# Last image in two token halves, filler products on PE in a bank of their own, and a new order of work

## Chip, cores and metric

The kernel runs on one core of a Trainium2 chip. The metric is device time in microseconds (us). Before the change the median of three runs is 472.86 us (471.47 to 474.82).

## The reference, cut to what matters

Four images of 16x16 tokens with 128 channels go through three layers one after another: a deformable attention layer, an attention layer over segments, and a layer of product-key experts. The change touches the end of the third:

```
s0 = einsum(l2norm(q0), l2norm(keys0)); s1 = the same with q1, keys1   # 8 heads, 64 keys a side
sc0, ix0 = top_k(s0, 16);  sc1, ix1 = top_k(s1, 16)
fs, pos  = top_k(all sums sc0 + sc1, 16);  fi = ix0 + ix1 at pos       # expert numbers below 128
w   = softmax(fs)
act = gelu(x . expert_down[fi])
out = sum over heads and k of act * w * expert_up[fi];   t = t + out
```

## The kernel before, in words

An image b has 256 tokens in two halves of 128 (t = 0, 1). Its work is cut into some sixty named stages (A: first layer, F: the rest of it and the second, N: experts). Each engine walks its own written list of `stage.image` (`ORDERS`, L108 to L142), strictly in order; images overlap because the lists interleave them. A stage on one engine waits on semaphores for what another engine made. Results of PE go into eight PSUM banks; the string `BANKS` (L154) gives each PE job its bank in the order of PE's list, and a job waits until the bank's last reader has freed it (`take`, L501).

Stages that the prediction speaks of:

- F7b: the layer norm statistics of the first layer's result (DVE L1172 and statistics), whose inverse root POOL takes (L1497). A2a to A2b2: POOL's multiplications and folds of the next image's convolution (L454, L1529).
- F9b, F9c: attention scores, four banks each, reduced by DVE (L1201). F10a, F10b: scores again, four banks each (PE L708), exponentials on ACT (L1003). F11a: the weighted sum (PE L721), F11t and F11b transposes, F11c projection. F5a: first-layer scores of the next image (PE L587). A1b: its query projection (PE L544).
- N0a, N0h: query projections of halves 0 and 1. N0b, N0d: their transposes (PE L520, ACT L1035). N0c, N0e: key scores (PE L775, ACT L1045). N1_0 to N1_3: the best keys on DVE (L1317 to L1327), two stages a half.
- N2a to N2f: the sixteen chosen pairs of each half. DVE sums and marks (L1365 to L1376) and masks (`chosen`, L1383 to L1389); POOL makes the sums of indices and of exponentials (`cells`) and merges the cells into 27 slots a head (`merge`, L1614 to L1620). L1389 multiplies 1/sum by 2^15.
- N3a: PE transposes the slots of both halves, weights (wT) and expert numbers (eT); ACT copies them (L1082, L1084); DVE splits the numbers in low and high bits (L1419, L1420), takes the remainder of the weights (L1425), makes four low masks (L1428) and four masked weight rows R (L1432). N3b: 32 masks of the high bits, 28 on DVE (L1437) and 4 on POOL (L1647).
- N5a, N5b: for each half PE adds the slots into experts, 128 pairs of a weight load (108x128, half precision) and a 16-column product (L839); DVE multiplies by the activations (L1442). N4 makes these activations. N6a: product with the up matrix (PE L850), ACT copy, N6b: transposes, the addition on DVE (L1459), and the store by DMA.

For the last image nothing of another image is left after N2f, so N3a to N6b run there one behind the other.

Of the kernel before, what the change touches and what calls it, by code (L numbers as in the profile page):

```python
# [52 lines left out]
POOL_HI = 4  # L53
W_SCALE = 2.0 ** 15
# [54 lines left out]
    "tensor": """A1a.0 A1b.0 A2d.0 A3a.0 A3b.0 A3c.0 A4.0 F5a.0 A1a.1 F5c.0 A1b.1 NS.0 F6a.0 F6b.0 F6c.0 F7a.0 F7b.0  # L109
        F8a.0 F8b.0 A2d.1 F9b.0 F9a.0 F8c.0 A3a.1 A3b.1 F9c.0 A3c.1 A4.1 F9d.0 F10a.0 F10b.0 F5a.1 F11a.0 A1a.2  # L110
        F11t.0 F11b.0 F11c.0 F5c.1 F12.0 N0a.0 F6a.1 N0h.0 F6b.1 A1b.2 N0b.0 F6c.1 N0c.0 N0d.0 N0f.0 F7a.1 F7b.1
        F8a.1 F8b.1 F8c.1 F9b.1 N0g.0 N0e.0 F9a.1 N4.0 A2d.2 A3a.2 F9c.1 A3b.2 F9d.1 A3c.2 F10a.1 A4.2 F10b.1
        F11a.1 F5a.2 F11t.1 F11b.1 F11c.1 N3a.0 F12.1 F5c.2 N0a.1 N0h.1 F6a.2 A1a.3 F6b.2 F6c.2 N0b.1 N0c.1
        N0d.1 N5a.0 N0e.1 F7a.2 N0f.1 F7b.2 N0g.1 N5b.0 F8a.2 F8b.2 A1b.3 F8c.2 F9b.2 F9a.2 F9c.2 A2d.3 N4.1
        N6a.0 F9d.2 A3a.3 A3b.3 A3c.3 F10a.2 F10b.2 F11a.2 A4.3 F11t.2 N6b.0 F11b.2 F5a.3 F11c.2 N3a.1 F5c.3
        F12.2 N0a.2 N0h.2 F6a.3 F6b.3 N0b.2 F6c.3 N0f.2 N0c.2 N0d.2 N0e.2 N5a.1 F7a.3 F7b.3 N5b.1 F8a.3 N4.2
        F8b.3 N0g.2 F8c.3 F9b.3 F9a.3 N6a.1 F9c.3 F9d.3 F10a.3 F10b.3 F11a.3 N6b.1 F11t.3 F11b.3 F11c.3 N3a.2
        F12.3 N0a.3 N0h.3 N0b.3 N0c.3 N0f.3 N5a.2 N0d.3 N0e.3 N0g.3 N5b.2 N6a.2 N4.3 N6b.2 N3a.3 N5a.3 N5b.3
        N6a.3 N6b.3""".split(),
    "scalar": """A0b.0 A1a.0 A2c.0 A2d.0 A3a.0 A1b.0 A3b.0 A3c.0 A4.0 A0b.1 F5b.0 A1a.1 F5c.0 F6b.0 F7a.0 F7b.0 A2c.1  # L120
        F8a.0 F8b.0 A1b.1 A2d.1 F9a.0 A3a.1 A3b.1 A3c.1 A4.1 A0b.2 F8c.0 F10a.0 F10b.0 F11t.0 A1a.2 F11b.0 F5b.1
        F12.0 F5c.1 N0a.0 F6b.1 N0h.0 N0b.0 N0c.0 F7a.1 F7b.1 N0d.0 F8a.1 F8b.1 A2c.2 F8c.1 N2p.0 A2d.2 F9a.1
        N0e.0 A3a.2 A3b.2 A3c.2 N2q.0 A1b.2 F10a.1 A4.2 F10b.1 F11t.1 F11b.1 N3a.0 F5b.2 F12.1 F5c.2 N0a.1 N0h.1
        A0b.3 F6b.2 N0b.1 N0c.1 N0d.1 A1a.3 N4.0 F7a.2 N0e.1 F7b.2 F8a.2 F8b.2 F8c.2 F9a.2 A2c.3 A2d.3 N2p.1
        A3a.3 A3b.3 A3c.3 F10a.2 F10b.2 N2q.1 A1b.3 F11t.2 N6a.0 A4.3 F11b.2 F5b.3 N3a.1 F12.2 F5c.3 N0a.2 N0h.2
        F6b.3 N0b.2 N0c.2 N0d.2 N4.1 F7a.3 F7b.3 N0e.2 F8a.3 N4.2 F8b.3 F9a.3 N2p.2 N2q.2 F10a.3 F8c.3 F10b.3
        N6a.1 F11t.3 F11b.3 N3a.2 F12.3 N0a.3 N0h.3 N0b.3 N0c.3 N0d.3 N0e.3 N2p.3 N2q.3 N6a.2 N4.3 N3a.3 N6a.3""".split(),
    "vector": """A0a.0 A2c.0 A3a.0 NB.0 A0a.1 F5a.0 NS.0 F6a.0 F6c.0 F7b.0 A2c.1 F8b.0 F9b.0 F9a.0 F9c.0 A0a.2 F9d.0
        F5a.1 A3a.1 F11a.0 F11c.0 N0a.0 F6a.1 N0b.0 N0h.0 F6c.1 N0d.0 N1_0.0 F7b.1 N1_1.0 A2c.2 N0f.0 F8b.1
        F9b.1 A3a.2 N2a.0 N2b.0 N1_2.0 F9a.1 N0g.0 F9c.1 N1_3.0 F9d.1 N2d.0 N2c.0 N2e.0 N2f.0 F11a.1 A0a.3 F5a.2  # L130
        F11c.1 N3a.0 N3b.0 N0a.1 F6a.2 N0h.1 N0b.1 N0d.1 F6c.2 N1_0.1 N1_1.1 N0f.1 N1_2.1 F7b.2 N2a.1 N2b.1
# [1590 lines left out]
```

## Time and profile before

| what | value |
|---|---|
| median of 3 runs | 472.86 us |
| profiled execution | 472.43 us, of it the span 470.6 us |
| PE busy | 296.5 us, 63% |
| weight loads on PE | 219.8 us, 47% |
| DVE busy | 356.8 us, 76% |
| ACT busy | 137.3 us, 29% |
| POOL busy | 220.8 us, 47% |
| granted PE clock, mean | 0.675 |
| chain that ended last | DVE 49%, PE 33%, ACT 7%, issue 5%, POOL 5% |

The span is the profiled stretch on the core; 1.8 us of the execution lie outside it. A busy share is an average over stages with different limits, so the rows further down are read stage by stage. The granted clock is 1.00 for 2.4 GHz and 0.50 for 1.2 GHz. The chain is followed back from the last instruction, at each step to what released it.

### The profile page before, as it was taken

The page shows a single profiled execution, that of the slowest core. Times are in us where ns is not written, and L with a number is a line of the kernel's source. Part 1 is how long each engine was busy: PE and PEld are TensorE (multiplying, and loading weights), DVE is VectorE, ACT ScalarE, POOL GpSimd, SP SyncE. Part 2 cuts the span into 40 slices and gives each one's busy share as a digit, 9 for nine tenths or more (in the row PEclk, how much of TensorE's full clock was granted, in tenths as well). Part 3 has the DMA queues.
Part 4 walks back from the last instruction along what each step waited for, and adds up shares of the span by engine and source line. Part 5 has one row for each costly group of instructions (what it writes and reads, how often), then busy time and mean ns, then how long its engine had stood idle before and what let it go on. Part 6 is the DMA issues. An engine that isn't in the chain of part 4 may idle for free.

```text
span 470.6 us, 7700 instructions
## 1 busy us (share of the span) xinstructions
PE 296.5 (63%) x2233; PEld 219.8 (47%) x2233; DVE 356.8 (76%) x2124; ACT 137.3 (29%) x320; POOL 220.8 (47%) x407
## 2 busy tenths in 40 slices
...
DMA packets 1633, 3.50 MB, mean 7 GB/s; under 512 B 180, under 2 KB 1205, under 8 KB 1592
## 3 DMA queue, kind: packets, MB, share of 16 engines
...
q8 instruction: 18, 0.29, 0.3%
...
HBM read 2.49 MB, written 0.52 MB: 6 GB/s over the span
## 4 chain that ended last, share of the span: by engine, by line
DVE 49%; PE 33%; ACT 7%; issue 5%; POOL 5%; DVEq 0%; ACTq 0%; POOLq 0%
PE bank L839 9%; DVE cands L1376 4%; DVE segmax L1201 4%; PE bank L520 4%; DVE onehot L1437 3%; DVE Sx L1320 3%; PE bank L755 3%; PE bank L775 3%; DVE i L1326 3%; DVE i L1327 3%; DVE c L1373 3%; DVE vraw L1323 2%; DVE rtm L1193 2%; DVE vraw L1317 2%; PE bank L608 2%
## 5 line engine op out<-in xcount | busy, mean ns | idle before, releaser
L839 PE MATMUL bank<-weights,onehot 108*128 108x16 f16 x1024 | 68.6, 216 | 18.5 <-DVE onehot L1437 13.0
L839 PEld LDWEIGHTS bank<-weights,onehot 108*128 108x128 f16 x1024 | 68.7, 175 | 19.4 <-DVE onehot L1437 13.5
L1584 POOL TENSOR_TENSOR inv<-nrm,mhalf 128x16 f32<-128x16 f32 x8 | 24.2, 3019 | 46.9 <-DVE nrm L1333 46.8
L454 POOL TENSOR_TENSOR taps<-qpad,wa 128x128 f32<-128x128 f32 x96 | 35.9, 425 | 17.4 <-ACT qpad L892 17.4
L1497 POOL TENSOR_TENSOR rstd<-veps,mhalf 128x2 f32<-128x2 f32 x16 | 11.7, 729 | 44.0 <-DVE veps L1123 43.7
L1647 POOL TENSOR_SCALAR onehot<-eT 108x512 f16<-108x512 uint16 x16 | 30.2, 1888 | 4.2 <-DVE eT L1420 3.5
L1437 DVE TENSOR_SCALAR onehot<-eT 108x512 f16<-108x512 uint16 x112 | 28.1, 327 | 0.0
L1326 DVE FIND_INDEX8 i<-vraw,S 128x8 uint16<-128x64 f32 x128 | 28.0, 219 | 0.0
L1327 DVE FIND_INDEX8 i<-vraw,Sx 128x8 uint16<-128x64 f32 x128 | 28.0, 219 | 0.0
L708 PE MATMUL bank<-qB,kE 32*128 32x256 f32 x128 | 16.3, 663 | 18.0 <-ACT PT L1003 10.1
L775 PE MATMUL bank<-KB,qsT 128*128 128x256 f32 x64 | 24.4, 548 | 3.5 <-ACT qsT L1035 3.5
L1320 DVE MATCH_REPLACE8 Sx<-vraw,S 128x64 f32<-128x64 f32 x128 | 25.1, 209 | 0.0
L1573 POOL TENSOR_TENSOR qrstd<-ssq,mhalf 128x8 f32<-128x8 f32 x8 | 17.7, 2212 | 14.7 <-DVE ssq L1285 14.7
L1376 DVE MATCH_REPLACE8 cands<-c,cands 128x54 f32<-128x54 f32 x128 | 23.7, 199 | 0.0
L520 PE MATMUL bank<-wa,hat 128*128 128x128 f32 x24 | 7.4, 406 | 24.8 <-ACT hat L877 24.6
L1317 DVE MAX8 vraw<-S 128x8 f32<-128x64 f32 x128 | 17.7, 213 | 6.3 <-ACT S L1045 6.3
L1201 DVE TENSOR_REDUCE segmax<-bank 128x32 f32<-128x512 f32 x32 | 19.8, 681 | 2.5 <-PE bank L678 2.4
L775 PEld LDWEIGHTS bank<-KB,qsT 128*128 128x128 f32 x64 | 17.2, 283 | 8.1 <-ACT qsT L1035 4.9
L1602 POOL TENSOR_TENSOR weights<-ab 128x64 f32<-128x64 f32 (+3 forms) x40 | 12.6, 348 | 17.9 <-ACT ab L1065 17.9
L1529 POOL TENSOR_TENSOR taps<-taps 128x1536 f32<-128x1536 f32 (+3 forms) x12 | 20.6, 1714 | 0.6
L1442 DVE TENSOR_TENSOR masked<-bank,act 128x512 f32<-128x512 f32 x8 | 8.4, 1072 | 16.0 <-PE bank L839 15.9
L708 PEld LDWEIGHTS bank<-qB,kE 32*128 32x128 f32 x128 | 10.0, 319 | 22.1 <-issue 12.0
...
## 6 DMA issues: line engine op xcount, KB each, us to landing
...
bq_row<-rows_dram SPq DMA_DIRECT2D x1, 0.5 KB
...
```

Source lines behind the costliest of these rows:

```text
L454: ins = eng.tensor_tensor(tv[:, :, :, ky, kx:kx + n], q, dw[:, ky, kx:kx + n].unsqueeze(1).unsqueeze(1).broadcast_to([P, G8, G8, n]), ALU. ...
L708: last = mm(banks[i][:, kc * N:kc * N + N], kE[r, j, kc * P:kc * P + P], qB[r, j, :], start=True, stop=True)
L775: last = mm(o[:, i * 256:i * 256 + 256], qsT[:, t, 2 * j + i, :], KB[:, :], start=True, stop=True)
L839: last = mm(o[:, g * 16:g * 16 + 16], OHv[:, c * NT + t, g], Rv[:, c, t, g, s], start=(c == 0 and s == 0), stop=(c == NCH - 1 and s == 1))
L1201: freed(v.tensor_reduce(segmax[:, t * H + i:t * H + H:4, :], o[:, :].rearrange("p (g n) -> p g n", n=SEG), X, ALU.max), job, b)
L1317: last = v.max(vt[:, g, 0:8], sv[:, g, :])
L1320: last = v.match_replace(sx[:, g, :], vt[:, g, 0:8], sv[:, g, :], MARK)
L1326: v.max_index(it[:, g, 0:8], vt[:, g, 0:8], sv[:, g, :])
L1327: last = v.max_index(it[:, g, 8:16], vt[:, g, 8:16], sx[:, g, :])
L1376: last = v.match_replace(dst[:, g, :], c8[:, g, i, :], src[:, g, :], MARK)
L1437: last = v.tensor_scalar(OH[0:KC, :, :, hi, :], hi_view(eT), float(LO * hi), None, ALU.is_equal)
L1647: last = g_.tensor_scalar(OH[0:KC, :, :, hi, :], hi_view(eT), float(LO * hi), None, ALU.is_equal)
```

## The change

1. All four lists are written anew; the stages are the same but for the additions. Among the moves: on PE, F5a.1 goes from before F11a.0 to behind F11t.0, A1a.2 from before F11t.0 to behind F11c.0, A1b.2 from before N0b.0 to behind F9b.1, N0d.3 from behind N5a.2 to before it, N5b.1 to directly behind N5a.1. On ACT, F8c.0 goes before the stage A4.1 and A0b.2 behind F11t.0. On POOL, F7b.0 goes before the last folds A2b2.1. On DVE, N5b.2 goes before N2a.3 and N6b.2 before N2e.3.
2. `W.0` to `W.20` in PE's list: two products each of 128x128 by 512 columns in bf16 of a tile of ones, into bank 7, which nobody reads. The other jobs get banks 0 to 6.
3. For the last image N3a and N3b do token half 0 alone; the new N3h and N3i do half 1. On PE N3h stands before N5a.3; on POOL the order is N3b.3, N2f.3 (the merge of half 1), N3i.3. The rows R of a half are eight operations of 256 columns in place of four of 1024.
4. The scale 2^15 moves from L1389, which goes, into ACT's copy and DVE's remainder, an operation that each does already.
5. `prod`, which DVE writes at L1442 and PE streams at L850, is laid out as DVE reads its operands; PE now reads it with a step of 16 elements.

```
-        f"... F9d.0 F10a.0 F10b.0 F5a.1 F11a.0 A1a.2 F11t.0 F11b.0 F11c.0 F5c.1 F12.0 N0a.0 ..."
+        f"... W.7 W.8 F8c.0 F9d.0 W.9 F10a.0 F10b.0 F11a.0 F11t.0 F5a.1 F11b.0 F11c.0 A1a.2 F5c.1 F12.0 N0a.0 ..."
...
+        "N5a.2 N0f.3 N0e.3 W.15 N5b.2 N0g.3 W.16 N6a.2 W.17 N4.3 N6b.2 N3a.3 N3h.3 N5a.3 W.18 N5b.3 W.19 W.20 N6a.3 N6b.3"
...
+            def W(k):
+                if k == 0:
+                    pe.wait_ge(preset, 1)
+                for _ in range(FILL):                     # FILL = 2
+                    mm(psum[7][:, :], ones3[:, :], ones3[:, :].unsqueeze(1).broadcast_to([P, 4, P]), start=True, stop=True)
...
+        def first_halves(b):
+            return list(range(NT)) if b < B - 1 else [0]
...
             def F8c(b):
                 o = take("v1", b)
+                read_out(pe, "tT", b)
...
+            def slot_transposes(b, halves, job):
+                pe.wait_ge(slots_ready, NT * b + halves[-1] + 1)
+                for kind, src in (("w", wn[:, :, :]), ("e", slots[:, 1, :, :])):
+                    transposes(kind + job, b, [
+                        ((c * NT + t) * P, src[:, t * H + c * HC:t * H + (c + 1) * HC, :].rearrange("p h s -> p (h s)"))
+                        for c in range(NCH) for t in halves])
...
             def N5b(b):
+                if b == B - 1:
+                    pe.wait_ge(onehot_dve_ready, b + 2)
+                    pe.wait_ge(onehot_pool_ready, b + 2)
                 scatter(b, 1)
...
+                pv = prod[:, :, :, :].rearrange("p t g (q l) -> p l t q g", q=4)
-                    last = mm(o[:, 0:N], up[:, lo, :], prod[:, lo], start=(lo == 0), stop=(lo == LO - 1))
+                    last = mm(o[:, 0:N], up[:, lo, :], pv[:, lo], start=(lo == 0), stop=(lo == LO - 1))
...
-                link(v.reciprocal(zs[:, 1, h], zs[:, 0, h]))
-                v.tensor_scalar(zs[:, 2, h], zs[:, 1, h], W_SCALE, None, ALU.mult).then_inc(wem_ready, 1)
+                v.reciprocal(zs[:, 1, h], zs[:, 0, h]).then_inc(wem_ready, 1)
...
+            def slot_rows(b, halves, job):                # DVE, in place of the body of N3a
+                ...
+                for lo in range(LO):
+                    if len(halves) == NT:
+                        v.tensor_tensor(R[0:KC, :, lo, :], W2[0:KC, :, :],
+                                        lom[0:KC, lo, :].unsqueeze(1).broadcast_to([KC, 2, NCH * N]), ALU.mult)
+                    else:
+                        for s in range(2):
+                            v.tensor_tensor(part(R[0:KC, s, lo, :], halves), part(W2[0:KC, s, :], halves),
+                                            part(lom[0:KC, lo, :], halves), ALU.mult)
...
                 freed(v.tensor_tensor(
-                    prod[:, :, t, :, :].rearrange("p l q g -> p g q l"),
-                    o[:, :].rearrange("p (g q l) -> p g q l", g=32, q=4), act[:, t, :, :, :], ALU.mult), f"G{t}", b)
+                    prod[:, t, :, :], o[:, :].rearrange("p (g e) -> p g e", g=32),
+                    act[:, t, :, :, :].rearrange("p g q l -> p g (q l)"), ALU.mult), f"G{t}", b)
...
+            def N3i(b):                                   # POOL; DVE's has hi from POOL_HI to HI
+                pool.wait_ge(eT_ready, b + 2)
+                for hi in range(0, POOL_HI):
+                    last = masks(g_, hi, [1])
+                last.then_inc(onehot_pool_ready, 1)
```

## Rows read from the trace of the kernel before

**Rows 1.** Windows of all engines: window, us, busy (count) of PE, PEld, DVE, ACT, POOL, clock

```profile
0.00:120.00 120.00, 66.25 (x316) 41.73 (x316) 62.61 (x246) 45.11 (x110) 65.03 (x129) 0.79 0.06 21
120.00:430.00 310.00, 207.06 (x1644) 157.04 (x1645) 279.39 (x1838) 90.65 (x207) 149.46 (x274) 0.65 0.01 3
430.00:470.60 40.60, 23.19 (x274) 21.06 (x273) 14.79 (x42) 1.58 (x3) 6.35 (x4) 0.50 0.01 4
```

**Rows 2.** Timeline of the head: start, us, engine, line, operation [idle before it]

```profile
55.64 1.55 DVE L1172 TENSOR_TENSOR t<-gl,z 128x256 f32<-128x256 f32 x1 [5.12 <-ACT gl L963]
80.42 0.88 ACT L877 ACTIVATE hat<-x_sb,shift,rstd 128x128 f32<-128x128 f32 x2 [5.61 <-POOL shift L1498]
83.01 4.03 ACT L1003 ACTIVATE PT<-bank 128x512 f32<-128x512 f32 x8
83.86 2.92 PE L587 MATMUL bank<-kBD,qhT 128*128 128x512 f32 x4
106.11 1.06 PE L544 MATMUL bank<-qT,wa 128*128 128x256 f32 x2
```

**Rows 3.** Timeline of DVE near 306: L1172 without POOL's folds beside it

```profile
306.72 0.42 DVE L1172 TENSOR_TENSOR t<-gl,z 128x256 f32<-128x256 f32 x1 [0.52 <-ACT gl L963]
```

**Rows 4.** Windows with the clock: the head's cold stretch, and inside a scatter

```profile
46.50:65.20 18.70, 8.52 (x25) 5.41 (x26) 4.77 (x17) 5.68 (x11) 12.48 (x20) 0.50 0.00 1
206.00:210.00 4.00, 4.00 (x63) 4.00 (x63) 3.97 (x39) 1.88 (x6) 3.84 (x11) 0.50 0.01 4
```

**Rows 5.** Timeline 379 to 393: last image's half 1 queries

```profile
379.29 8.56 PE L839 MATMUL bank<-weights,onehot 108*128 108x16 f16 x128 [5.51 <-issue]
388.83 0.78 ACT L1035 ACTIVATE qsT<-bank,wb 128x512 f32<-128x512 f32 x1 [15.20 <-PE bank L520]
392.46 1.11 DVE L1317 MAX8 vraw<-S 128x8 f32<-128x64 f32 x8 [4.50 <-ACT S L1045]
```

**Rows 6.** Lines L1442, L1291, L1389 alone: count, ns min/median/max, starts

```profile
L1442 DVE TENSOR_TENSOR masked<-bank,act x8: 1010/1042/1191, 232.1 to 461.8; 128x512 f32<-128x512 f32 x8
L1291 DVE TENSOR_TENSOR queries<-bank,qrstd x8: 672/682/692, 104.0 to 380.2; 128x512 f32<-128x512 f32 x8
L1389 DVE TENSOR_SCALAR zs<-zs x8: 170/171/260, 168.2 to 426.5; 128x8 f32<-128x8 f32 x8
```

**Rows 7.** Timeline of the tail: from the last merge to the product with the up matrix

```profile
426.69 0.53 POOL L1614 COPY slots<-masked 128x16 f32<-128x16 f32 x3 [0.74 <-DVE zs L1389]
429.21 0.55 POOL L1620 TENSOR_TENSOR wn<-slots,zs 128x216 f32<-128x216 f32 x1
432.56 0.29 DVE L1419 TENSOR_SCALAR eT<-eT 108x512 uint16<-108x512 uint16 x1 [5.60 <-ACT eT L1084]
435.02 3.26 DVE L1432 TENSOR_TENSOR weights<-W,cands 108x1024 f16<-108x1024 f16 x4
438.20 6.55 DVE L1437 TENSOR_SCALAR onehot<-eT 108x512 f16<-108x512 uint16 x28
444.80 16.98 PE L839 MATMUL bank<-weights,onehot 108*128 108x16 f16 x256 [13.04 <-DVE onehot L1437]
462.95 3.75 PE L850 MATMUL bank<-masked,up 128*128 128x256 f32 x8 [1.16 <-issue]
```

**Rows 8.** Timeline of DVE: eight searches over 54 columns

```profile
421.84 1.01 DVE L1373 MAX8 c<-cands 128x8 f32<-128x54 f32 x8
```

**Rows 9.** Timeline: DVE's masks and POOL side by side, image 2 and last image

```profile
364.87 1.64 POOL L1573 TENSOR_TENSOR qrstd<-ssq,mhalf 128x8 f32<-128x8 f32 x1 [5.36 <-DVE ssq L1285]
367.00 6.22 POOL L1573 TENSOR_TENSOR qrstd<-ssq,mhalf 128x8 f32<-128x8 f32 x1 [0.49 <-DVE ssq L1285]
367.44 5.74 DVE L1437 TENSOR_SCALAR onehot<-eT 108x512 f16<-108x512 uint16 x28
433.21 6.54 POOL L1647 TENSOR_SCALAR onehot<-eT 108x512 f16<-108x512 uint16 x4 [3.46 <-DVE eT L1420]
```

**Rows 10.** Waits of PE after 120 us: us in total, times, longest

```profile
PE bank L708 <- ACT PT L1003: 10.1, 3, 7.8
```

More of the change, by code:

```diff
@@ L53 @@
 POOL_HI = 4
+FILL = 2
 W_SCALE = 2.0 ** 15
@@ L108 @@
 ORDERS = {
[L109 to L118, printed above, removed]
-        N6a.3 N6b.3""".split(),
@@ L120 @@
[L120 to L131, printed above, removed]
-        N0g.1 A2c.3 N5a.0 N5b.0 F8b.2 F9b.2 F9a.2 F9c.2 N2c.1 F9d.2 N1_3.1 N2d.1 N2e.1 F11a.2 N2f.1 N6b.0 F5a.3
-        F11c.2 N3a.1 N0a.2 N0h.2 F6a.3 N0b.2 N3b.1 N0d.2 F6c.3 N1_0.2 N1_1.2 N5a.1 F7b.3 N0f.2 N1_2.2 N2a.2
-        N5b.1 N2b.2 F8b.3 F9b.3 F9a.3 F9c.3 N0g.2 N2c.2 F9d.3 A3a.3 N1_3.2 N2d.2 N2e.2 N2f.2 N6b.1 F11a.3 F11c.3
-        N3a.2 N0a.3 N0h.3 N0b.3 N3b.2 N1_0.3 N0d.3 N1_1.3 N1_2.3 N0f.3 N5a.2 N1_3.3 N0g.3 N2a.3 N5b.2 N2d.3
-        N2b.3 N2c.3 N2e.3 N2f.3 N6b.2 N3a.3 N3b.3 N5a.3 N5b.3 N6b.3""".split(),
@@ new lines @@
+    "vector": """A0a.0 A2c.0 A3a.0 NB.0 A0a.1 F5a.0 NS.0 F6a.0 F6c.0 F7b.0 A2c.1 F8b.0 F9b.0 F9a.0 F9c.0 F9d.0 A0a.2
+        F11a.0 F5a.1 F11c.0 N0a.0 F6a.1 N0b.0 N0h.0 F6c.1 N0d.0 N1_0.0 N1_1.0 N1_2.0 N0f.0 F7b.1 N1_3.0 A2c.2
+        N2a.0 N0g.0 F8b.1 F9b.1 F9a.1 F9c.1 N2b.0 F9d.1 N2d.0 N2c.0 N2e.0 N2f.0 F11a.1 F5a.2 A0a.3 F11c.1 N3a.0
+        N3b.0 N0a.1 F6a.2 N0h.1 N0b.1 N0d.1 F6c.2 N1_0.1 N1_1.1 N0f.1 N1_2.1 F7b.2 N2a.1 A2c.3 N5a.0 N2b.1 N5b.0
+        F8b.2 F9b.2 F9a.2 F9c.2 N2c.1 N0g.1 F9d.2 N1_3.1 N2d.1 N2e.1 F11a.2 N2f.1 F5a.3 N6b.0 F11c.2 N3a.1 N0a.2
+        N0h.2 A3a.1 F6a.3 N0b.2 N3b.1 A3a.2 N1_0.2 N0d.2 F6c.3 N0f.2 A3a.3 N1_1.2 N5a.1 N2a.2 N5b.1 F7b.3 N1_2.2
+        F8b.3 N2b.2 N0g.2 F9b.3 F9a.3 F9c.3 N2c.2 F9d.3 N1_3.2 N2d.2 N2e.2 N2f.2 F11a.3 N6b.1 F11c.3 N3a.2 N0a.3
+        N0h.3 N0b.3 N3b.2 N0d.3 N1_0.3 N1_1.3 N0f.3 N1_2.3 N1_3.3 N0g.3 N5a.2 N5b.2 N2a.3 N2d.3 N2b.3 N2c.3
+        N6b.2 N2e.3 N2f.3 N3a.3 N3b.3 N3h.3 N3i.3 N5a.3 N5b.3 N6b.3""".split(),
```

132 lines of the change are left out of this document (85 added, 47 removed).

## The prediction

> **What bounds the kernel now.** I read the shares first, then the windows, because DVE's 76% is an average over three very different stretches [rows 1]. Up to 120 us DVE is busy for 62.6 us: only image 0 and the front of image 1 are there, and their stages follow each other across the engines. From 120 to 430 us DVE is busy 279.4 of 310 us, 90%: here DVE is the bound, and what is taken off it or closes one of its gaps counts. From 430 us to the end it is 14.8 of 40.6 us: one image, one chain. So I read each stretch by another question: what stands ahead of the next link (head), what DVE does or waits for (middle), how much of the chain can run beside itself (tail).
>
> **Head.** (a) The addition L1172 of image 0 takes 1.55 us while POOL folds, 0.42 us without folds [rows 2, 3]. With F7b.0 ahead of the last folds, POOL stands idle meanwhile: 1.1 us less. The folds end some 3 us later; their reader on DVE stands before F8b.0, which waits for two more steps on ACT and PE, so they stay hidden. (b) ACT begins the exponentials of F10a.0 at 83.01, behind a layer norm of another image at 80.42 (0.88) and then 1.7 us of F8c's copy and a table load [rows 2]. In the new list both stages are away, and the load falls in an idle time. At most 2.6 us are to be had; PE's own products then come last, so I take 1.6 for the exponentials, which end near 85.5 instead of 87.0. F5a.1 (2.92 us, until 86.8) is no longer before F11a.0 either, and F11a.0 ends 2.0 us earlier. (c) A1a.2 leaves the place before F11t.0 (0.6 us) and A1b.2 that before N0b.0 (1.06 us [rows 2], 0.85 of it in the way); F5a.1 now stands between F11t.0 and F11b.0, in a gap that I estimate at 0.8 us, and costs 1.2 (warm) to 2.1 (cold); I take 1.6. Net 0.1 lost. (d) The fillers. They matter if they keep the clock at 1.00. From 46.5 to 65.2 us PE is busy 8.52 us at 0.50, on the chain [rows 4]; at full clock that is at best half, 4.2 us less. W.4 and W.5 stand before F6c.0, behind a step of ACT of half a us, and are four products of 512 columns, 0.85 us warm and 1.7 cold at a column a cycle of the granted clock. So (d) lies between 3.4 gained and 1.3 lost; I take 1.5 gained, since no row shows how soon they act. Head: 1.1 + 2.0 - 0.1 + 1.5 = **4.5 us**.
>
> The rest of the fillers I cost at nothing before the tail: W.0 to W.3, W.6 to W.8 and W.10 to W.17 stand before products that wait longer than the 0.85 us that a pair takes cold. Where that cover is missing a pair costs 0.85.
>
> Here a rule disagrees with a row. The clock is 0.50 from 206 to 210 us although PE's records fill all 4.0 us with 16-column products [rows 4]: being busy did not keep the clock. The Trainium skill ("TensorE: Matmul & The Clock Gate", What's actually happening) says that the default is throttled and activity releases it. By that rule alone all fillers pay and (d) is 3.4; the row says that the kind of work counts, so I do not take it whole.
>
> **Middle.** DVE's product L1442 writes scattered and takes 1.04 us; L1291, the same shape from PSUM with a packed output, 0.68 [rows 6]. I price the packed L1442 at 0.68: 0.36 off each, six in this stretch, 2.2 us (at worst nothing, if the scattered write is not the reason). L1389 (0.17 and its hand-over, 0.2 together) goes seven times before the last: 1.4 us. The scale moves into operations that exist, at no cost. Before the last image's N1_2, DVE stands idle 4.50 us, since N0d.3 starts behind the scatter that ends at 387.85; that scatter itself had waited 5.51 us [rows 5]. With N0d.3 before N5a.2 the transposes and ACT's copy fall into that wait, and the time from 387.85 to the copy's end at 389.61 goes: 1.8 us. Middle: 2.2 + 1.4 + 1.8 = **5.4 us**. The remaining moves shuffle work under a busy DVE; N5b.1 right behind N5a.1 makes F7a.3 and N0e.2 wait 8.6 us longer, but DVE has N1_1.2, N2a.2 and two products, over 12 us, ahead of them. I take zero for them, bounds 5 either way: DVE's idle time in this stretch is 30 us, most of it the small gaps between instructions.
>
> **Tail.** Before, N2f ends, POOL merges from 426.69 to 429.76, PE and ACT bring the slots to DVE at 432.56; DVE needs until 444.75 (2.46 for the first seven operations, 3.26 for R, 6.5 for the masks), PE 17.0 for both scatters, and from the product L850 to the end of the span are 7.65 us [rows 7].
> Half 0's mask was done at 421.84 [rows 8], now some 0.7 earlier by a cheaper product and L1389; its merge takes 3.1 to 4 and is done by 425.3, the transposes take 1.0, the copies 0.6: DVE can start N3a.3 at 427.0, 5.5 us earlier. N6b.2's early place frees the buffer that ACT's copy needs.
> Half of it on DVE: a mask over half the columns lies between 0.10 and 0.205 us; eight searches over 54 columns take 1.01 us, 0.126 each [rows 8], so little below that is to be had: I take 0.14, 28 are 3.9. R as eight operations of 256 columns: 1.6 (a quarter each) to 3.2; 1.9. The first seven: 1.7. With 1.3 for POOL's interference: 8.8 us, ready at 435.8. The split is no saving on DVE, it is 5.4 us more work; what it buys is that the second half lies beside the first scatter.
> POOL: the four masks of N3b.3 now stand before the merge of half 1. Masks of half the size are half of 6.54, 3.3 us [rows 9], the merge 3.1 to 3.8: slots near 434.4, transposes until 435.4. PE has N3h.3 before N5a.3, so the scatter of half 0 waits for that too; it starts at 435.8 and ends at 444.3. Half 1's preparation runs 436.3 to 444.1 beside it. W.18 is then not covered: 0.85. Scatter 1 ends at 453.7. W.19 and W.20 are four products, 1.7 us cold, where PE waits 1.1 us: product L850 starts at 455.4. I give it no warm clock, since after 17 us of scatter it is 0.50 [rows 1]. With 7.65 to the end the span ends at 463.0: **7.6 us**.
>
> **Sum.** 4.5 + 5.4 + 7.6 = 17.5. The profiled execution took 472.43, 0.43 under the median; 472.43 - 17.5 = 454.9, against the median 455.4. I say 455.
>
> **Rivals.** (1) *POOL is shut out in the tail.* Beside 28 masks of DVE in 5.74 us, a POOL instruction of 1.6 us took 6.22 [rows 9]: DVE went at full speed and POOL stood. Against it: in the last image POOL's four masks ran 6.54 us and DVE was the slower. If DVE wins in the new tail, POOL does its masks after 433.8, the merge ends at 440.2, half 0's scatter starts at 441.2, half 1 is ready at 452.3, and the span ends at 470.2: the tail gives 0.4 instead of 7.6, **462 us**. The Trainium skill ("SBUF — State Buffer", SBUF: two separate sides) calls this port pair an exclusive lock that whoever starts first holds for its instruction. The rows show both outcomes, so it decides nothing between them.
> (2) *Product L850 becomes slow.* Its moving operand has a step of 64 bytes now. If each column then costs twice, the last one adds 3.75 us, the three others lie beside DVE: **459 us**. Against it: a scatter pair loads 128 weight columns of half precision, 64 bytes apart, and streams 16 more in 66 ns (8.56 us/128), 2 columns a ns, where L850 needs one in 1.8 ns. The Trainium skill ("SBUF — State Buffer", The DMA port swizzle) has a rule that speaks for it: lines of 16 bytes, and two hits a line are needed for full speed.
> (3) *The clock is kept.* Fillers hold it in the head and at the end: 1.9 more in (d), and 2 to 3 elsewhere in the head and at L850: **450 us**.
> (4) *Seven banks are too few: slower.* F10a and F10b need eight banks; today PE already waits up to 7.8 us for one held by ACT [rows 10]. With seven, the last product of F10b, or of F9c, waits for the first reader, which in the middle comes when its engine's list lets it, and everything behind on PE waits with it, N0 products for DVE too. At 7.8 us on DVE's path for each of images 1 to 3 that is 23.4 us: **478 us**. It outweighs the gains from 6 us an image on. Against it: DVE and ACT read these sets in a row, 0.6 us a bank, so the fourth waits little.
> (5) *The new order gives back the gains* by milder waits of the same sort, 4 us an image: **467 us**.
>
> **Numbers.** Forecast (451 to 459 with its own bounds) 0.45, (1) 0.15, (2) 0.10, (3) 0.12, (4) 0.06, (5) 0.12. Range 446 to 468: it takes in all but (4) and parts of the edges. A measurement of this kernel tells about 1% from no change, 468.1 and 477.6. Faster: all but (4) and half of (5), less a little of (1): 0.84. Same 0.10, slower 0.06.
>
> **What would show it.** Head: L1172 of image 0 at 0.42, first exponentials near 79 to 80 on the new time axis, first N1_0 some 5 us earlier; the clock between 45 and 65. Middle: L1442 at 0.7, the idle before N1_2.3 under 3 us, no long wait of PE for a bank. Tail: scatter of half 0 starting 9 us before today's 444.8, a gap under 1.5 us between the scatters, L850 at 3.75. I am wrong if DVE's idle time in the middle grows, if POOL's merge of half 1 lands after 437, or if L850 lengthens.

## The result, and the profile after

The changed kernel takes 451.19 us (median of 4 runs, 449.87 to 452.28) against 473.58 (471.47 to 474.82) for the kernel before in the same comparison: ratio 0.953, 95% interval 0.949 to 0.958. The prediction said 455 with a range of 446 to 468. The profiled execution took 449.87 us, of it the span 447.8: 22.8 us less than the 470.6 of before, where the sum had said 17.5.

Three stretches as in [rows 1]: cut at 120 us again, and at 415 us, which lies 3.2 us behind the last 1/sum (430 lay 3.8 us behind it). Busy times of the engines, then the granted clock.

```profile
0.00:120.00 120.00, 72.25 (x350) 46.11 (x350) 66.95 (x307) 45.72 (x112) 62.77 (x127) 0.82 0.06 21
120.00:415.00 295.00, 211.26 (x1649) 158.11 (x1649) 275.93 (x1781) 93.82 (x209) 147.14 (x269) 0.67 0.01 3
415.00:447.80 32.80, 24.60 (x276) 20.96 (x276) 15.56 (x77) 1.15 (x3) 7.97 (x17) 0.55 0.02 5
```

DVE is the bound of the middle still, now 94% busy instead of 90%; over the span its share went from 76% to 80%. To see where the 22.8 us came from I take two marks that exist in both traces: the first key search of image 0 on DVE (MAX8 of S), and the last 1/sum on DVE (before L1388, after L1431), with which N2f of the last half ends.

| stretch | before | after | gained | predicted |
|---|---|---|---|---|
| start to first key search | 111.54 | 105.38 | 6.2 | 4.5 |
| first key search to last 1/sum | 314.67 | 306.43 | 8.2 | 5.4 |
| last 1/sum to end of span | 44.39 | 35.99 | 8.4 | 7.6 |

The table compares one execution with one. In a second profiled execution of the changed kernel (e0 below) the same stretches gain 7.1, 7.0 and 8.5 us, so head and middle are known to about 1 us each.

**The tail** came as worked out. Timeline of the kernel after, columns: start, duration, engine, line, operation, in brackets the idle time before and what ended it. First POOL and DVE, then PE.

```profile
411.97 0.23 DVE L1459 TENSOR_SCALAR eT<-eT 108x256 uint16<-108x256 uint16 x1
413.54 2.04 DVE L1479 TENSOR_TENSOR weights<-W,cands 108x256 f16<-108x256 f16 x8
415.50 5.59 DVE L497 TENSOR_SCALAR onehot<-eT 108x256 f16<-108x256 uint16 x28
422.69 2.06 DVE L1479 TENSOR_TENSOR weights<-W,cands 108x256 f16<-108x256 f16 x8
424.67 4.21 DVE L497 TENSOR_SCALAR onehot<-eT 108x256 f16<-108x256 uint16 x28
```
```profile
412.50 3.80 POOL L497 TENSOR_SCALAR onehot<-eT 108x256 f16<-108x256 uint16 x4 [2.27 <-DVE eT L1460]
...
418.96 0.55 POOL L1680 TENSOR_TENSOR wn<-slots,zs 128x216 f32<-128x216 f32 x1
421.64 3.85 POOL L497 TENSOR_SCALAR onehot<-eT 108x256 f16<-108x256 uint16 x4 [2.12 <-DVE eT L1460]
```
```profile
421.14 8.62 PE L876 MATMUL bank<-weights,onehot 108*128 108x16 f16 x128 [0.47 <-DVE onehot L497]
429.61 1.01 PE L550 MATMUL bank<-ones 128*128 128x512 bf16 x2
430.41 8.64 PE L876 MATMUL bank<-weights,onehot 108*128 108x16 f16 x128
438.90 1.87 PE L550 MATMUL bank<-ones 128*128 128x512 bf16 x4
440.56 3.64 PE L888 MATMUL bank<-masked,up 128*128 128x256 f32 x8
```

DVE takes up half 0 at 411.97 and PE scatters it from 421.14: 9.2 us, predicted 8.8. The preparation of half 1 (421.18 to 428.9) lies under this scatter, so only the filler pair W.18 stands between the two scatters, a gap of 0.65 us. Before, DVE prepared both halves and then PE scattered both [rows 7].

**The head.** Windows with PE's busy time and the granted clock, and the products in them. First before, then after:

```profile
90.00:96.00 6.00, 3.00 (x19) 1.00 0.00 0
98.00:104.00 6.00, 6.00 (x21) 0.50 0.00 0
98.01 2.08 PE L755 MATMUL bank<-wb,fT 128*128 128x512 f32 x2
99.88 3.47 PE L608 MATMUL bank<-vBD,PT 128*128 128x34 f32 x16
```
```profile
90.00:96.00 6.00, 4.81 (x28) 1.00 0.00 0
98.00:104.00 6.00, 5.19 (x28) 1.00 0.00 1
97.01 1.94 PE L635 MATMUL bank<-vBD,PT 128*128 128x34 f32 x16
99.21 1.12 PE L783 MATMUL bank<-wb,fT 128*128 128x512 f32 x2
```

From 96 to 104 us the clock stood at 0.50 before and stands at 1.00 after; in the six us ahead of that PE was busy for 3.0 us there, 4.8 here. The same products take 2.08 and 1.12 us, 3.47 and 1.94. Just before 80 us nothing is gained at all: DVE starts to write qB, which the scores of F10a need, at 79.39 in the one and 79.42 in the other.

**The middle.** DVE's product (groups by shape: busy, mean ns of one | idle before), to be held against L1442 in [rows 6]:

```profile
L1502 DVE TENSOR_TENSOR masked<-bank,act 128x512 f32<-128x512 f32 x8 | 5.4, 684 | 9.6 <-PE bank L876 9.5
```

### The profile page after: what moved, and what is told of

Its sections match the earlier page's. It is cut to its first block, busy times and chain, and to the rows that moved or that the text cites. A ratio compares the mean times of both kernels' runs of the same rounds, so it can differ in the third digit from the quotient of the medians.

```text
span 447.8 us, 7841 instructions
## 1 busy us (share of the span) xinstructions
PE 308.1 (69%) x2275; PEld 225.2 (50%) x2275; DVE 358.4 (80%) x2163; ACT 140.7 (31%) x324; POOL 217.9 (49%) x411
## 4 chain that ended last, share of the span: by engine, by line
DVE 55%; PE 23%; POOL 9%; issue 6%; ACT 6%; DMA 1%; DVEq 0%; ACTq 0%; POOLq 0%
PE bank L876 6%; DVE Sx L1363 5%; DVE i L1369 5%; DVE i L1370 5%; DVE cands L1419 4%; DVE onehot L494 4%; DVE vraw L1366 3%; DVE vraw L1360 3%; DVE segmax L1244 3%; DVE c L1416 3%; PE bank L540 2%; PE bank L550 2%; DVE masked L1426 2%; PE bank L783 2%; ACT hat L914 2%
## 5 line engine op out<-in xcount | busy, mean ns | idle before, releaser
L1644 POOL TENSOR_TENSOR inv<-nrm,mhalf 128x16 f32<-128x16 f32 x8 | 23.4, 2925 | 35.8 <-DVE nrm L1376 35.8
L494 DVE TENSOR_SCALAR onehot<-eT 108x512 f16<-108x512 uint16 x84 | 24.4, 366 | 0.0
L1633 POOL TENSOR_TENSOR qrstd<-ssq,mhalf 128x8 f32<-128x8 f32 x8 | 13.7, 1714 | 19.4 <-DVE ssq L1328 19.3
L1040 ACT ACTIVATE PT<-bank 128x512 f32<-128x512 f32 x32 | 16.4, 611 | 21.1 <-PE bank L736 21.1
L494 POOL TENSOR_SCALAR onehot<-eT 108x512 f16<-108x512 uint16 x12 | 20.5, 1709 | 0.6
L540 PEld LDWEIGHTS bank<-wa,hat 128*128 128x128 f32 x24 | 3.1, 175 | 34.9 <-ACT hat L914 34.8
L736 PE MATMUL bank<-qB,kE 32*128 32x256 f32 x128 | 15.3, 616 | 6.4 <-ACT PT L1040 3.5
L1366 DVE MAX8 vraw<-Sx 128x8 f32<-128x64 f32 x128 | 17.8, 211 | 0.6
```

The lines of the kernel that those rows point to most:

```text
L494: return unit.tensor_scalar(OH[0:KC, :, :, hi, :], e.rearrange("p (n q g) -> p n q g", n=NCH * NT, q=4), float(LO * hi), None, ALU.is_equal)
L1366: last = v.max(vt[:, g, 8:16], sx[:, g, :])
L1644: g_.tensor_tensor(inv[:, n], nrm[:, n], mhalf[:, 0:2 * H], ALU.pow).then_inc(inv_ready, 1)
```

## The experiments

Twelve runs, in three batches (e1 to e4; e0, e5, e7, e12; e6, e9, e10, e11); each batch shared its runs of the kernel before (medians 474.57, 473.81 and 475.36), so totals are compared with care across batches and the ratios first. "Head", "middle" and "tail" are the three stretches of the table above, from each kernel's own profiled execution. Between executions of one kernel the total scatters by 2 to 6 us.

### The changed kernel again

The changed kernel without an edit, for the second batch.

> The changed kernel itself once more, as the yardstick for the kernels beside it: 451 us, ratio to before 0.953. Its trace also shows whether the short 1.77 us of POOL's second query root near 354 us comes back: in four other traces of nearly the same kernel this instruction took 6.22 us beside DVE's masks, and the scatter behind it started 2 to 3 us later. If that outcome is the usual one, DVE's idle before the last image's third search is 3 to 4.5 us here too, not 0.3.

450.22 us (448.57 to 451.96, 6 runs), ratio 0.950 [0.946, 0.954]. Head 104.4, middle 307.7, tail 35.9. The gain stands on a second chip. The short 1.77 us of POOL's second query root did not come back: it takes 6.22 us here, as in ten of the other kernels' traces and in the one of before, and DVE's idle time before N1_2.3 is 2.4 us instead of 0.3. Only the first trace (1.77) and e9 (1.64) have the short form.

### The fillers

```diff
# e1_no_fillers: PE's list without W.0 to W.20
-... A1b.0 W.0 W.1 A3a.0 ... N5a.3 W.18 N5b.3 W.19 W.20 N6a.3 N6b.3
+... A1b.0 A3a.0 ... N5a.3 N5b.3 N6a.3 N6b.3
# e2_no_tail_fillers: only W.18 to W.20 go
-N3h.3 N5a.3 W.18 N5b.3 W.19 W.20 N6a.3 N6b.3
+N3h.3 N5a.3 N5b.3 N6a.3 N6b.3
```

> The changed kernel (451.2 us, ratio to before 0.953) without any of the 42 filler products. Theory A, the fillers keep PE's clock and pay: the granted clock between 82 and 108 us, 1.00 in the changed kernel and mostly 0.50 to 0.6 before, falls back, the first search of keys on DVE moves from 105.4 to 108 or later, and the kernel takes 454 us or more. Theory B, the warm stretch comes from the denser order of the real products and the fillers only stand in the way: 0.8 us at W.4 and W.5, 1.0 at W.7 and W.8, 1.3 in the tail go, and the kernel takes 448 to 450 us.

> The changed kernel without W.18, W.19 and W.20 alone. By the prediction's working W.18 is not covered (0.65 us between the scatters) and W.19 and W.20 delay the product with the up matrix by 0.6 us: 449.9 us, ratio to before 0.950. If they warm the clock for that product (its last part of eight ran faster, 3.64 us against 3.75), 0.1 to 0.5 us of it comes back.

Without any: 451.83 us (450.57 to 455.15, 5 runs), ratio 0.951 [0.948, 0.953]. Without those of the tail: 449.95 us (6 runs), ratio 0.948 [0.945, 0.951]. With all: 0.950 and 0.953 in two batches. The intervals overlap, so the totals do not show what the fillers are worth. These two kernels, which share a batch, differ by W.0 to W.17 alone and by 1.9 us in the median. The traces tell more of the places. In the tail the fillers cost 1.1 to 1.2 us, since nothing covers them; end of the last scatter and product with the up matrix in the kernel without any, timeline of PE:

```profile
427.55 17.27 PE L875 MATMUL bank<-weights,onehot 108*128 108x16 f16 x256 [0.47 <-DVE onehot L496]
445.65 3.78 PE L887 MATMUL bank<-masked,up 128*128 128x256 f32 x8 [0.83 <-issue]
```

The scatters run without a gap, and the product starts 0.83 us after them instead of 1.51. Behind W.19 and W.20 it runs at a granted clock of 0.68 instead of 0.50, which is worth 0.14 us (3.78 to 3.64).

In the middle they pay, at one place. PE in N0a.2 (a query projection of image 2) and F6a.3 (L635, of image 3; both lines are seen in the head too), first in the changed kernel again (e0), then without any filler:

```profile
263.32 1.13 PE L783 MATMUL bank<-wb,fT 128*128 128x512 f32 x2 [0.22 <-ACT fT L1055]
265.66 1.87 PE L635 MATMUL bank<-vBD,PT 128*128 128x34 f32 x16
```
```profile
266.10 2.08 PE L782 MATMUL bank<-wb,fT 128*128 128x512 f32 x2
270.51 3.47 PE L634 MATMUL bank<-vBD,PT 128*128 128x34 f32 x16
```

The granted clock is 1.00 there with the fillers and 0.50 without. From the last key search of image 1 to the first of image 2 DVE needs 39.2 us in the one and 41.3 in the other. This repeats: 41.3 us in all three kernels without fillers (this one, e6, e10), 39.0 to 39.3 in eight traces with W.10 and W.11; the ninth, e4, has 40.5 us and the query projections at half clock. The nearest fillers ahead are W.10 and W.11, 14 to 15 us earlier; no run takes them out alone. So the fillers give some 2 us in the middle and take 1.2 in the tail; what they do elsewhere is open.

### The two token halves

```diff
         def first_halves(b):
-            return list(range(NT)) if b < B - 1 else [0]
+            return list(range(NT))
...
-  tensor: N3a.3 N3h.3 N5a.3    scalar: N3a.3 N3h.3    vector: N3b.3 N3h.3 N3i.3    gpsimd: N3b.3 N2f.3 N3i.3
+  tensor: N3a.3 N5a.3          scalar: N3a.3          vector: N3b.3                gpsimd: N2f.3 N3b.3
```

> The changed kernel with the last image's slots, masks and scatters prepared for both halves at once, as before, and POOL's merge of half 1 before its masks; all else is kept. Theory A, the split is worth what the prediction says: the time from DVE's last reciprocal to the end of the span goes from 36.0 back to 44 less 0.35 for the cheaper product, 43.7, and the kernel takes 458.5 to 459.5 us. Theory B, the gain of the tail comes from the moves around it (N6b.2's early place): under 455.

459.03 us (ratio 0.968 [0.964, 0.971]), 8 to 9 us more than the changed kernel, and the trace puts all of it into the tail: 45.1 against 36.0, while head and middle (104.8 and 307.8) are those of the changed kernel. Timeline of PE without the split:

```profile
431.02 8.62 PE L873 MATMUL bank<-weights,onehot 108*128 108x16 f16 x128 [13.04 <-DVE onehot L494]
```

PE stands for 13.0 us until DVE has masks and rows of both halves. With the split the first scatter starts 9.9 us earlier, at 421.14, and the second half's preparation lies under it.

### The layout of the product before the up matrix

```diff
# e4_scattered_product: the changed kernel, written as before
-        prod = masked[...].rearrange("p (t g e) -> p t g e", t=NT, g=32)
+        prod = masked[...].rearrange("p (l t q g) -> p l t q g", l=LO, t=NT, q=4)
-                pv = prod[:, :, :, :].rearrange("p t g (q l) -> p l t q g", q=4)
-                    last = mm(o[:, 0:N], up[:, lo, :], pv[:, lo], ...)
+                    last = mm(o[:, 0:N], up[:, lo, :], prod[:, lo], ...)
-                    prod[:, t, :, :], o[:, :].rearrange("p (g e) -> p g e", g=32),
-                    act[:, t, :, :, :].rearrange("p g q l -> p g (q l)"), ALU.mult), ...)
+                    prod[:, :, t, :, :].rearrange("p l q g -> p g q l"),
+                    o[:, :].rearrange("p (g q l) -> p g q l", g=32, q=4), act[:, t, :, :, :], ALU.mult), ...)
# e12_read_with_step, against e4: DVE writes packed for PE, and reads bank and act with a step; ACT's copy puts the columns back
+        prod = masked[...].rearrange("p (l t e) -> p l t e", l=LO, t=NT)
+                    prod[:, :, t, :], o[:, :].rearrange("p (e l) -> p l e", l=LO),
+                    act[:, t, :, :, :].rearrange("p g q l -> p l (g q)"), ALU.mult), ...)
# e11_step_16_bytes: the changed kernel, other order of PE's columns; ACT's copy puts them back
-                pv = prod[:, :, :, :].rearrange("p t g (q l) -> p l t q g", q=4)
+                pv = prod[:, :, :, :].rearrange("p t g (q l) -> p l t g q", q=4)
```

> The changed kernel with the old layout of the product tile: DVE writes it scattered, PE streams it packed. Theory A, the scattered write is what made DVE's product 1.04 us: it goes from 0.68 back to 1.02 to 1.04, eight times, and the kernel takes 2 to 2.8 us more, 453.5 us; the product with the up matrix stays at 3.6 to 3.75 us. Theory B, streaming with a step of 64 bytes costs PE something: that product gets shorter than 3.64 and the kernel is not slower.

> The changed kernel with the product tile packed for PE's stream and for DVE's write, and the step of four elements put on DVE's reads (PSUM and activations); ACT's copy puts the columns back in order. In the traces so far the product with the up matrix took 3.6 to 3.8 us with the 64 byte step at either clock (3.69 and 3.61 at granted clock 1.00), and 1.89 to 1.99 with a packed stream at 1.00. Theory A, the stream's step is the floor: at clock 1.00 it takes 1.9 to 2.0 again, and the last one, half warm, 2.8: 0.9 us less in the tail. If DVE's reads with a step are free, the kernel takes 450.3 us; if they cost what the scattered write did (1.04), 452.5.

> The changed kernel with PE reading the product before the up matrix in another order of columns: the step between neighbouring columns is 16 bytes instead of 64, and ACT's copy puts the columns back in place. PE streams 8 products of 256 columns here: with a step of 64 bytes 3.6 to 3.8 us at either clock, packed 1.9 at full clock and 3.7 cold. If the rate hangs on the size of the step (a line that a column touches alone), a step of 16 bytes gives something between, 1.9 to 2.7 at full clock; if any step is enough to lose the fast rate, 3.6 again at full clock. Cold it is 3.7 in both. Total by either 450 (449 to 451.5), since the products of images 0 to 2 lie beside DVE and the last one runs cold; ACT's copy with a step may add 0.3 once.

Scattered write: 452.94 us, ratio 0.954 [0.951, 0.957]. Read with a step: 452.37 us, 0.955 [0.950, 0.960]. Step of 16 bytes: 450.82 us, 0.950 [0.945, 0.955]. Against the 0.950 and 0.953 of the changed kernel these totals differ by less than the intervals can tell; what is sure is in the rows. DVE's product in the first and in the second (groups by shape):

```profile
L1501 DVE TENSOR_TENSOR masked<-bank,act 128x512 f32<-128x512 f32 x8 | 8.3, 1052 | 9.1 <-PE bank L876 9.0
```
```profile
L1501 DVE TENSOR_TENSOR masked<-bank,act 128x512 f32<-128x512 f32 x8 | 8.5, 1076 | 9.1 <-PE bank L876 9.0
```

So the 0.37 us a piece (0.39 in the second) are DVE's price of a step, and it is nearly the same whether the written side has it (256 elements between neighbours) or the read side (4 elements). What does the step cost on PE's side? The products of 256 columns of one image, eight records, their busy time on PE in a window around them, and the granted clock (third number from the end; the four products of an image are eight records): first the changed kernel at either clock (second batch), then the scattered product, then the step of 16 bytes.

```profile
313.40:317.10 3.70, 3.61 (x8) 1.46 (x8) 1.00 0.00 0
394.00:397.90 3.90, 3.78 (x8) 2.36 (x8) 0.50 0.00 0
```
```profile
317.10:319.10 2.00, 1.89 (x8) 1.42 (x8) 1.00 0.00 0
445.30:448.20 2.90, 2.76 (x8) 1.94 (x8) 0.69 0.00 0
```
```profile
314.30:318.20 3.90, 3.81 (x8) 1.67 (x8) 0.94 0.00 0
```

Packed, they take 1.9 us at full clock and 3.75 at half [rows 7]. With a step of 64 bytes they take 3.6 at full and 3.8 at half clock; the clock hardly matters any more. A step of 16 bytes is as slow, so of the two outcomes that its expectation named, the second came. Smaller steps than 16 bytes were not tried. The kernel that reads with a step (e12) says nothing on the packed rate at full clock: its products ran at 0.50 to 0.58 in all four images and took 3.2 to 3.75 us. In the tail the changed kernel's last product has a clock of 0.68 (0.66 in e0), so the step costs 0.9 us there (3.63 against the 2.76 of the scattered kernel's last), and DVE's gain, 0.37 us for each of eight products, pays for it.

### The two small edits alone, on the kernel before

```diff
# e5_before_two_edits
-        prod = masked[...].rearrange("p (l t q g) -> p l t q g", l=LO, t=NT, q=4)
+        prod = masked[...].rearrange("p (t g e) -> p t g e", t=NT, g=32)
...
-                v.tensor_scalar(zs[:, 2, h], zs[:, 1, h], W_SCALE, None, ALU.mult).then_inc(wem_ready, 1)
-                link(fn(W2[0:KC, 0, :], o[0:KC, :], ACT.Copy))
+                link(fn(W2[0:KC, 0, :], o[0:KC, :], ACT.Identity, scale=W_SCALE))
-                freed(v.tensor_tensor(W2[0:KC, 1, :], o[0:KC, :], W2[0:KC, 0, :], ALU.subtract), "wT", b)
+                freed(v.scalar_tensor_tensor(W2[0:KC, 1, :], o[0:KC, :], W_SCALE, W2[0:KC, 0, :], ALU.mult, ALU.subtract), "wT", b)
```

> The kernel before with two edits of the change alone: the packed product tile, and the scale moved out of DVE's last small operation. Prediction: 8 products at 0.36 and 8 operations at 0.2, 4.4 us of DVE's work, of which nearly all lies where DVE is the bound: 469.5 us. A rival: the work goes but the gaps grow by as much, under 2 us gained.

469.94 us against 473.81: 3.9 us, ratio 0.993 [0.989, 0.996], so this gain is clear of the scatter. The terms of the sum for these two edits were 2.2 + 1.4 in the middle and 0.7 in the tail, 4.3 together.

### N0d.3 behind the scatter again

```diff
-N0c.3 N0d.3 N5a.2 N0f.3
+N0c.3 N5a.2 N0d.3 N0f.3
```

> The changed kernel with the transposes N0d.3 put back behind the scatter N5a.2 on PE. Theory A, the move is worth the 1.8 us that the prediction took from the rows of before: 453.0 us against 451.2. Theory B, DVE's wait was set by POOL's masks and the scatter's start, not by the transposes: within 0.7 us of the changed kernel.

452.96 us (ratio 0.955 [0.950, 0.960]) against 450.22: 2.7 more, with a term of 1.8; each of its four runs is slower than each of the six of the changed kernel. DVE before N1_2.3, the first key search of the last image's half 1, first with N0d.3 early (e0), then with it late:

```profile
378.41 1.11 DVE L1360 MAX8 vraw<-S 128x8 f32<-128x64 f32 x8 [2.43 <-ACT S L1082]
```
```profile
381.78 1.12 DVE L1360 MAX8 vraw<-S 128x8 f32<-128x64 f32 x8 [3.26 <-ACT S L1082]
```

The search comes 3.4 us later, but that of N1_0.3, ahead of the edit, comes 1.7 us later already (361.81 against 360.08): 1.6 us lie here. In the profiled executions 2.1 us of the difference lie in the head, which the edit does not touch, so of the 2.7 only the 1.6 are shown to be its work. With N0d.3 early DVE still waits 2.43 us, since the scatter whose masks are shown further down starts late.

### The new orders alone

```diff
# e10_orders_only: no W.k, the halves as in e3, the product as in e4
```

> The changed kernel without its three separable parts: no filler products, no token halves in the last image, and the product before the up matrix written scattered as before (1.04 us instead of 0.69). Left of the change are the four new lists, the seven banks and the scale that moves into operations that exist. My theory: the parts add. Without the split the kernel took 459.0 us, the scattered product costs 2.7 us more, the fillers are worth nothing over the whole, so this one takes 461.5 (460 to 463), and against 473.8 before the lists and the scale alone are worth some 12 us: 5 in the head, the rest in the middle, of which 1.8 are N0d.3 and 1.4 the scale. First key search of image 0 near 106.5, tail near 45. Rival, rival (5) of the prediction in another form: the lists gain nothing by themselves and the other parts need them: 468 or more.

463.51 us (461.29 to 464.02, 4 runs), ratio 0.975 [0.970, 0.980]: 2 us over what I expected, with the fillers put at nothing (compare their 2 us in the middle), and 11.9 us under the kernel before. Head 105.1, tail 44.0. So the gain of 6.2 us in the head is there to the full without a single filler, and so is the clock; windows of PE as above:

```profile
84.00:90.00 6.00, 4.95 (x34) 0.81 0.01 3
90.00:96.00 6.00, 4.81 (x26) 1.00 0.00 0
98.00:104.00 6.00, 5.19 (x28) 1.00 0.01 1
```

DVE starts to write qB at 77.28 here, 2.1 us earlier than in the changed kernel's trace. There the addition of F7b.0, behind W.4 and W.5, came 0.8 us later (56.44 against 55.67), and behind W.7 and W.8 PE began the transposes for qB 1.0 us after DVE had written their operand. With the fillers the clock is 1.00 from 84 to 90 us too, where it is 0.81 here, and by 87.5 both stand nearly level (transposes of F11t at 87.48 and 87.73). In this pair of traces the fillers take 2 us in the head and give them back. Over all traces the difference drowns: qB is started between 77.10 and 80.65 in eight with all fillers of the head, at 77.28, 77.33 and 78.81 in the three without.

### The eighth bank

```diff
# e6_no_fillers_8_banks: e1, with bank 7 for the last product of F9c and of F10b
-BANKS = """0123456012453601245360124536024251346046025130...
+BANKS = """0123456012453601245360124536024251746046025130...
```

> The changed kernel without fillers, and with the eighth bank given to the last product of F9c and of F10b in each image, which have to wait for one of seven banks otherwise. To be compared with the kernel without fillers on seven banks, 451.8 us. My theory: the bank is not missed, 451.5 (450.5 to 452.5): the waits of PE for these banks are 3.5 us in the whole middle and DVE has work meanwhile. Rival, rival (4) of the prediction: the seventh-bank wait is on the path in each image, and the bank gives back 2 to 6 us: 446 to 449.5.

451.65 us (4 runs), ratio 0.950 [0.945, 0.955], against 451.83 and 0.951 [0.948, 0.953] with seven banks. The bank is not missed.

### A better version

```diff
# e9_fewer_fillers_n0d_first: without W.4 W.5 W.7 W.8 W.18 W.19 W.20, and
-tensor: N0c.3 N0d.3 N5a.2 N0f.3 N0e.3 W.15     vector: N0b.3 N3b.2 N0d.3 N1_0.3
+tensor: N0c.3 N0d.3 N0e.3 N5a.2 N0f.3 W.15     vector: N0b.3 N0d.3 N3b.2 N1_0.3
```

> A try at a better version: the changed kernel without the fillers W.4, W.5, W.7, W.8 (which stood ahead of products that could have started: 0.8 and 1.0 us in the head) and W.18 to W.20 (1.2 us in the tail), and with N0d.3 ahead of N3b.2 on DVE and N0e.3 ahead of N5a.2 on PE, so that the key scores of the last image stand ready before the scatter. Expected: 1.2 from the tail, 1 from the head if the other fillers keep the clock there, 1 to 2 from the scores: 447.5 (446 to 450). If the fillers' clock in the head is lost with these four, the head gives nothing: 449. If N0d.3 takes from N3b.2 what it gives to the scores, the scatter starts as much later and N0d.3 brings nothing: 449 too.

449.78 us (448.59 to 450.46, 6 runs), ratio 0.947 [0.943, 0.950]. It is the lowest ratio of all, but its interval overlaps that of the changed kernel; no version here is shown to be better. The tail is 1.1 us shorter (34.8). The middle is 1.4 longer (309.1), and the trace shows why the second edit brings nothing. Masks of image 2 on POOL and DVE and the scatter that waits for them, first in the changed kernel (second batch), then here:

```profile
353.22 6.22 POOL L1633 TENSOR_TENSOR qrstd<-ssq,mhalf 128x8 f32<-128x8 f32 x1 [0.61 <-DVE ssq L1328]
353.65 5.74 DVE L494 TENSOR_SCALAR onehot<-eT 108x512 f16<-108x512 uint16 x28
354.82 10.58 POOL L494 TENSOR_SCALAR onehot<-eT 108x512 f16<-108x512 uint16 x4
365.51 8.56 PE L876 MATMUL bank<-weights,onehot 108*128 108x16 f16 x128 [4.64 <-issue]
```
```profile
357.17 8.58 DVE L494 TENSOR_SCALAR onehot<-eT 108x512 f16<-108x512 uint16 x28
356.50 7.09 POOL L494 TENSOR_SCALAR onehot<-eT 108x512 f16<-108x512 uint16 x4
365.80 8.62 PE L876 MATMUL bank<-weights,onehot 108*128 108x16 f16 x128 [0.68 <-DVE onehot L494]
```

Above, DVE's masks run at full speed and are done at 359.4; POOL, in its root since 353.22, gets on only then and finishes the masks at 365.4. Below, DVE reaches its masks 3.5 us later, since N0d.3 ahead of them waits for this root; both engines then run at once, DVE's 28 masks take 8.58 us, and all end by 365.75. So the scatter starts at the same time (365.5 and 365.8), the wait of 2.43 us before N1_2.3 is gone, but DVE's first key search begins at 365.67 instead of 360.08, and N1_2.3 itself 1.5 us later. The equal start of the scatter comes from the late start of DVE's masks. The first trace of the changed kernel shows the two engines at once with the masks in their old place:

```profile
354.33 8.99 DVE L494 TENSOR_SCALAR onehot<-eT 108x512 f16<-108x512 uint16 x28
355.50 7.28 POOL L494 TENSOR_SCALAR onehot<-eT 108x512 f16<-108x512 uint16 x4
```

All masks are there 9.0 us after DVE's first one, instead of 11.8 (353.65 to 365.4), and DVE is free 3.2 us later.

## Why the prediction was right, and where its sizes were off

**Head, F7b.0** (gain 1.1). The addition takes 0.43 us instead of 1.55, as the step said. But nothing of it reaches the path: at 79.4 us both traces stand level. Timeline of the kernel after:

```profile
75.76 1.91 PE L550 MATMUL bank<-ones 128*128 128x512 bf16 x4
77.47 1.06 PE L688 MATMUL bank<-wb,tlT 128*128 128x128 f32 x4
...
79.42 0.69 DVE L1262 TENSOR_TENSOR qB<-bank,q1P 128x512 f32<-128x512 f32 x1 [2.14 <-PE bank L540]
81.78 4.03 ACT L1040 ACTIVATE PT<-bank 128x512 f32<-128x512 f32 x8 [1.00 <-PE bank L736]
```

W.7 and W.8 end at 77.67 and F8c.0 at 78.5, and only then PE turns to the transposes for qB, whose operand DVE had ready at 77.27. The prediction had put these fillers, like W.4 and W.5, at nothing, since the products behind them would wait longer. They did not: 1.0 us here, and 0.8 at W.4 and W.5 by the comparison with the orders-only kernel, where DVE starts qB at 77.28. The gain of F7b.0 and of PE's order is there (2.1 us), and in this trace the fillers ate it.

**Head, exponentials** (gain 2.0). They start 1.2 us earlier (81.78 against 83.01 [rows 2]) and end at 85.8; I had said 85.5, with a term of 1.6. The term is near. But the sign "first exponentials near 79 to 80" failed in this trace, since it counts on (a) and on the clock before 65 us as well, and the sum over both steps is short: F11a.0 ends 1.6 us earlier (88.65 and 87.02), where (a) and (b) together had said 3.1.

**Head, the clock** (gain 1.5, bounds 3.4 gained to 1.3 lost). This is the term that was mis-sized, and for the wrong cause. The clock stayed at 0.52 from 45 to 65 us, where I had looked for the gain. It stayed at 1.00 from 96 to 104 us, where before it had fallen to 0.50 and where I had not looked: the two pairs of L783 (0.96 us less each) and L635 (1.5 less) take 3.5 us less. And the kernels without fillers show that these have no part in it: 1.00 from 98 to 104 us in all three. In the new order PE is busy for 4.8 us of the 6 from 90 to 96 us instead of 3.0 (4.8 to 5.3 in all twelve traces of the new order, 3.0 in the two of the old), and the clock is kept. That this is the cause is argued from the windows; no run changed it alone. The Trainium skill ("TensorE: Matmul & The Clock Gate", What's actually happening) says that activity releases the throttle, and these windows agree with it; the prediction had weighed that rule for the fillers alone. That the head came out near (4.5 said, 6.2 measured) is in part luck: the 1.1 of (a) and the 1.5 of (d) did not arrive in this trace, the fillers cost what the sum had put at nothing, and 3.5 us came from a place that was no term of it.

**Middle** (gain 5.4, measured 8.2, and 7.0 in the second execution). The product and the scale: 3.6 + 0.7 predicted for the whole kernel, 3.9 measured alone. N0d.3: 1.8 predicted, 1.6 by the marks of the trace, 2.7 by the medians. What is left, 2 to 3 us, is a second term that was mis-sized: W.10 to W.17 stood in the sum at nothing. The stretch between two key searches shown above is 2 us longer in all three kernels without fillers; whether the orders give anything beyond that in the middle stays open. DVE's waits in the whole middle are 20.6 us before, 12.7 and 17.0 in the two traces of the changed kernel, and 22.3 to 24.0 in the three kernels without fillers. The profiled executions of two of these three were the slowest of their runs (455.15 of 450.57 to 455.15, and 453.38 of 449.67 to 453.38), so a whole middle of 311.5 or 312.9 us against 306.4 to 308.3 proves little; the third, the orders-only kernel, lies at its median (463.54, and 463.51) and shows the same 41.3 us and the same waits. By the medians all fillers together give 0.6 or 1.6 us (451.83 against 451.19 and 450.22), which no interval here can tell from nothing.

**Tail** (gain 7.6, measured 8.4). From DVE's first operation on half 0 to the end: 36.0 predicted, 35.8 measured. The preparation of a half was 9.2 instead of 8.8, half 1's merge ended 7.5 us after the start (7.4 predicted), and product L888 to the end took 7.2 instead of 7.65. W.18 to W.20 cost 1.2 us where the sum had 0.85 + 0.6. These deviations nearly cancel and leave 0.2 of the extra 0.8. The other 0.6 lies ahead of them: the prediction had DVE start half 0 at 427.0, 0.8 us after the last 1/sum of before (426.21), and it starts 0.16 us after its own (411.81), since half 0's slots were there by then.

**The rivals.** (1) POOL was not shut out in the tail: its four masks began at 412.50, three us ahead of DVE's, and took 3.80 us, and the merge of half 1 followed at once and was done at 419.5. DVE paid, with POOL at work beside most of its 28 masks: 5.59 us against 4.21 in half 1, where POOL was idle after 425.5. At the masks of image 2 it did go the other way in all traces but two (6.22 us for one L1633), as before. (In the working of this rival DVE's masks end, by its own terms, at 427.0 + 1.7 + 1.9 + 3.9 = 434.5 and not at 433.8.) (2) The step costs a factor of two, but only against a full clock (3.61 against 1.89 us); at the clock that the last product has, it cost 0.9 us. The rule of the Trainium skill ("SBUF — State Buffer", The DMA port swizzle) that a line of 16 bytes has to be hit twice for full speed agrees with these rows: at a step of 64 bytes and at one of 16 each column touches a line of its own, and both are slow. But the sentence behind that rule gives four float32 as a distance that one can still step for free, and four float32 are the 16 bytes that took 3.81 us here against 1.89 packed: there the measurement decides. Nor does it say that this pace is slower than a full clock only. (3) The clock kept: it came in part, in the head by the order and not by the fillers (3.5 us), in the middle by the fillers (2 us); no other term is as much above the sum, so these are the likely reason why it was 451 and not 455. (4) Seven banks: refuted by the eighth, for the two products that the rival names. (5) Gains given back: none seen; the orders with the scale are worth 11.9 us.

The parts add up within their scatter: orders and scale 11.9, halves 8 to 9, product 2 to 3, fillers 0 to 2, together 22 to 26. Measured are 22.4 and 23.6 us in the two comparisons of the whole.
